# Moving part of a layer norm to GpSimd, one sum to VectorE, and the order of two stretches of work

## The reference, cut to what matters

```python
def _layernorm(x, axis=-1, eps=1e-05): ...          # no gain, no bias
def _binary_diff_weight(w, base):
    d = w - base
    coeff = jnp.mean(jnp.abs(d))                     # one number for the whole matrix
    return base + coeff * jnp.sign(d)
# FFN branch: 1792 inner columns in 14 chunks of 128
gate, up = xn @ W1.T, xn @ W3.T;  g = silu((silu(gate) * up) @ W2.T)
# attention-like branch: weights NF4[codes] * scales, rank 16 additions (LoRA)
attn = (q + k + v) / 3;  x1 = xn + o(attn);  s = x1 + down(silu(gate(x1)) * up(x1))
return x + s * g                                     # x: 1024 tokens x 512
```

## Time and profile before

| | |
|---|---|
| runs | 536.11, 536.21, 536.38 us; median 536.21 |
| the profiled execution | 536.4 us, span 534.6 us |
| PE busy | 522.1 us of the span, 98% |
| VectorE, ScalarE, GpSimd busy | 83%, 61%, 18% |
| mean granted clock of TensorE | 0.997 |
| PE's longest waits | 4.7, 1.7, 1.1, 0.9, 0.6 us |

### The profile page before, as it was taken

How to read it: one execution, slowest core, us unless ns; L and a number is a source line. 1 busy time by engine, 2 the same in 40 slices (tenths; PEclk the granted TensorE clock), 3 DMA queues, 4 the chain that set the end, 5 groups by cost and what they waited for, 6 DMA issues and landing times.

```text
span 534.6 us, 6499 instructions
## 1 busy us (share of the span) xinstructions
PE 522.1 (98%) x2337; PEld 432.2 (81%) x2337; DVE 442.0 (83%) x520; ACT 328.5 (61%) x455; POOL 94.8 (18%) x106
## 2 busy tenths in 40 slices
PE   5899999999999999999999999999999999999997
PEld 4678888888888888888888888887888888888886
DVE  6988998988896998865898988999989898874446
ACT  2979978557546555446648557867876585464310
POOL 1311002003100310022003121300310040004590
PEclk9899999999999999999999999999999999999999
DMA  8999904045811491059238994932582377127503
GB/s 337 397 402 403 377 4 154 25 132 99 189 50 63 70 229 58 1 104 224 51 75 159 243 219 100 195 83 63 97 163 58 75 157 148 29 51 161 135 20 139
DMA packets 31744, 76.73 MB, mean 144 GB/s; under 512 B 3872, under 2 KB 7296, under 8 KB 31584
## 3 DMA queue, kind: packets, MB, share of 16 engines
q1 hardware_dynamic: 21632, 57.42, 34.4%
q0 software_dynamic: 9792, 18.88, 20.4%
q10 hardware_dynamic: 288, 0.02, 0.0%
HBM read 53.23 MB, written 2.10 MB: 103 GB/s over the span
## 4 chain that ended last, share of the span: by engine, by line
PE 87%; DVE 8%; issue 3%; DMA 1%; ACT 1%; SPq 0%; DVEq 0%; ACTq 0%
PE up_ps L1692 25%; PE gate_pair L1692 22%; PE down_pair L1733 10%; PE up_ps L1733 9%; PE down_ps L1733 7%; PE side_ps L1776 2%; PE down_pair L1692 2%; DVE acc L1339 2%; PE down_pair L1645 1%; PE up_ps L1853 1%; PE gate_pair L1853 1%; PE down_pair L1853 1%; DMA xn<-in_x 1%; PE down_pair L1815 1%; PE gate_pair L1733 1%
## 5 line engine op out<-in xcount | busy, mean ns | idle before, releaser
L1692 PE MATMUL up_ps<-xT,gu 128*128 128x512 f32 x648 | 152.3, 390 | 0.4 <-DVE gu L1173 0.2
L1692 PE MATMUL gate_pair<-xT,gu 128*128 128x512 f32 x624 | 148.4, 390 | 0.0
L1692 PEld LDWEIGHTS up_ps<-xT,gu 128*128 128x128 f32 x648 | 121.4, 188 | 26.4 <-DVE gu L1173 0.6
L1692 PEld LDWEIGHTS gate_pair<-xT,gu 128*128 128x128 f32 x624 | 117.0, 188 | 24.6 <-DVE gu L1164 0.5
L651 POOL DMA_DIRECT2D y<-y_part x64 | 55.3, 875 | 339.9 <-ACT y_part L815 338.7
L802 ACT ACTIVATE h<-up_ps 128x512 fp32r<-128x512 f32 x52 | 31.0, 597 | 111.1 <-DVE up_ps L1231 58.0
L861 ACT ACTIVATE ramp<-codes,bend_bias 128x1536 f32<-128x1536 uint8 x56 | 88.1, 1579 | 0.9 <-DMA codes<-in_codes 0.9
L1339 DVE SCALAR_TENSOR_TENSOR acc<-ramp,acc 128x1536 f32<-128x1536 f32 x42 | 73.7, 1754 | 4.4 <-ACT ramp L861 4.0
L1733 PE MATMUL down_pair<-h,dn 128*128 128x512 f32 x249 | 60.9, 389 | 0.0
L1733 PEld LDWEIGHTS down_pair<-h,dn 128*128 128x128 f32 x249 | 46.7, 188 | 9.8
L1236 DVE TENSOR_TENSOR h<-up_ps,h 128x512 fp32r<-128x512 f32 x52 | 35.8, 689 | 19.7 <-ACT h L802 19.4
(11 more groups left out here) (227 smaller groups left out, 648.1 us busy)
## 6 DMA issues: line engine op xcount, KB each, us to landing
y<-y_part POOLq DMA_DIRECT2D x64, 256.0 KB, 5.0
scale<-in_scales SPq DMA_DIRECT2D x28, 384.0 KB, 5.5
scan_w<-in_w SPq DMA_DIRECT2D x15, 512.0 KB, 10.9
base<-in_mean SPq DMA_DIRECT2D x9, 768.0 KB, 4.8
scan_mean<-in_mean SPq DMA_DIRECT2D x9, 512.0 KB, 9.7
silu_gate<-in_mean SPq DMA_DIRECT2D x6, 512.0 KB, 12.2
codes<-in_codes SPq DMA_DIRECT2D x14, 192.0 KB, 5.6
xn<-in_x SPq DMA_DIRECT2D x4, 512.0 KB, 4.9
```

The lines of the kernel that those rows point to most:

```text
L1692: last = nc.tensor.matmul(ps[:, :], w[:, w_part, hc * P:(hc + 1) * P], xT[:, x_part, hc, th * HALF:(th + 1) * HALF], start=(hc == 0 and w_ ...
```

## The change

GpSimd normalises x tiles 4 to 7, after its copy of `next_gate` and ahead of `early_low`; it waits for the tenth `ln_step` and counts on a semaphore of its own. Scan tile 2 is summed by VectorE (`scan_sum(2)`) instead of ScalarE (`sum_apart(2)`). VectorE does scan tiles 0 and 1 back to back, then all eight low tiles. ScalarE makes the high part of the early base weight before the first scan tile. On PE the warm-up transposes have other counts and places, both halves of `early_signs` stand ahead of the first `total`, and chunk 2 of gate is made earlier. Late in the kernel, chunk 18's orders on VectorE and ScalarE change.

```diff
-DVE_SUMS = [4, 6, 8, 9, 12]
+DVE_SUMS = [2, 4, 6, 8, 9, 12]
-SUM_FIRST = [2, 3, 13]
+SUM_FIRST = [3, 13]
-WARM = {-1: 12, 1: 8, 3: 5, 7: 7}
+WARM = {-1: 8, 1: 8, 3: 7}
+WARM_LOW = {1: 3, 2: 3, 3: 3}
+WARM_TOTAL = [5, 8]
+H_AHEAD = [18]
+RANK_AHEAD = [18]
@@ GpSimd
+            pool.wait_ge(ln_step, 10)
+            for t in range(HC, TT):
+                nc.gpsimd.tensor_scalar(xn[:, t, :], xn[:, t, :], moments[:, t, 0:1], inv_std[:, t:t + 1],
+                                        ALU.subtract, ALU.mult).then_inc(xn_ready_pool, 1)
             early_low()
@@ ScalarE
+                if k in RANK_AHEAD:
+                    split(k)
                 steps(k, 1, 0, 1)
...
+                    if stage == "D4" and t == 6:
+                        y_evict(g, t)
+                        steps(stage, 1, 3, 4)
+                        continue
...
+            early_high()
             scan_signs(0)
-            early_high()
...
-            sum_apart(2)
...
+            unit_high(2)
             unit_signs(3)
             silu(0, 0)
-            unit_high(2)
@@ VectorE, phase(k)
+                if k - 1 in H_AHEAD:
+                    h_low(k - 1, 1)
+                    third_scale(k - 1)
...
+                if k in RANK_AHEAD:
+                    for s in NF4_STEPS[k - 1][1][2:3]:
+                        nf4_bend(s)
+                        nf4_scale(s)
+                else:
+                    rank_part(k)
...
+                if k in H_AHEAD:
+                    h_make(k, 1)
...
+                if k + 1 in RANK_AHEAD:
+                    rank_part(k + 1)
@@ VectorE, head
             scan_subtract(0)
-            for t in range(4, TT):
-                normalise(t)
             scan_subtract(1)
-            for t in range(4):
+            for t in range(TT):
                 x_low(t)
-            x_low(4)
-            x_low(5)
             scan_subtract(2)
-            x_low(6)
-            x_low(7)
+            scan_sum(2)
...
             early_scale(0)
+            unit_make(2)
             early_add(0)
             early_scale(1)
-            unit_make(2)
+            unit_low(2)
             early_add(1)
             scan_subtract(5)
-            unit_low(2)
@@ PE
+            pe.wait_ge(ln_step, 1)
             warm(side_ps, WARM[-1])
             for t in range(TT):
-                pe.wait_ge(xn_ready, t + 1)
+                if t < HC:
+                    pe.wait_ge(xn_ready, t + 1)
+                else:
+                    pe.wait_ge(xn_ready_pool, t - HC + 1)
...
-            pe.wait_ge(xT_lo, 1)
-            warm(early_ps[0], WARM[TT - 1])
+            for low, count in WARM_LOW.items():
+                pe.wait_ge(xT_lo, low)
+                warm(early_ps[0], count)
...
             early_signs(0)
+            early_signs(1)
+            warm(gate_ps[1], WARM_TOTAL[0])
             total(GATE)
-            early_signs(1)
+            warm(gate_ps[1], WARM_TOTAL[1])
```

More of the change, by code:

```diff
@@ L340, in block_kernel @@
         xn_ready = sem("xn_ready")
+        xn_ready_pool = sem("xn_ready_pool")
         xT_tr = sem("xT_tr")
@@ L883, in phase @@
                     silu(k, 0)
-                    split(k)
+                    if k not in RANK_AHEAD:
+                        split(k)
                 steps(k, 1, 1, 2)
@@ L928, in down_stage @@
                             dn_high(SPLIT_IN[stage])
-                    else:
+                    elif stage != "D4" or t != 5:
                         steps(stage, 1, t - 2, t - 1 if t < TT - 1 else None)
@@ L1377, in phase @@
             def phase(k):
-                if BEFORE[k] == k - 1:
+                if k - 1 in H_AHEAD:
+                    h_low(k - 1, 1)
+                    third_scale(k - 1)
+                elif BEFORE[k] == k - 1:
                     h_make(k - 1, 1)
-                    third_scale(k - 1)
+                    if k not in RANK_AHEAD:
+                        third_scale(k - 1)
                 make(k)
                 steps(k, 0)
-                if BEFORE[k] == k - 1:
+                if BEFORE[k] == k - 1 and k - 1 not in H_AHEAD:
                     h_low(k - 1, 1)
@@ L1386, in phase @@
                     dn_low(k)
-                rank_part(k)
+                if k in RANK_AHEAD:
[4 more added lines that the diff above has]
+                    rank_part(k)
                 if k == FIRST:
@@ L1395, in phase @@
                     return
-                steps(k, 1, 0, 1)
-                split(k)
+                if k in RANK_AHEAD:
+                    split(k)
+                    steps(k, 1, 0, 1)
+                else:
+                    steps(k, 1, 0, 1)
+                    split(k)
                 steps(k, 1, 1, 2)
@@ L1402, in phase @@
                     h_low(k, 0)
+                if k in H_AHEAD:
+                    h_make(k, 1)
                 for s in ATTN_STEPS[k][1][2:3]:
                     attn_step(s)
-                for s in NF4_STEPS[k][1][2:3]:
-                    nf4_bend(s)
+                if k + 1 in RANK_AHEAD:
+                    rank_part(k + 1)
+                else:
+                    for s in NF4_STEPS[k][1][2:3]:
+                        nf4_bend(s)
                 if k - 1 not in LATE_PHASES:
```

## The result

The changed kernel takes 542.48 us (542.29 to 543.36, 4 runs) against 536.16 (536.08 to 536.38, 4 runs): a ratio of 1.0121 [1.0106, 1.0135], 6.3 us slower. The forecast was 535.9, the range 534.6 to 537.6.

The account below looks back on a forecast made before the run. PE, which never pauses once chunk 1 of gate starts at 32.01, was taken as the bound. 536.4 + 0.1 (head) - 0.2 - 0.2 (two gaps) = 536.1, the median 0.2 below: 535.9 us, range 534.6 to 537.6.

Parts of the forecast that it names:

- The price of the normalise: Head, GpSimd: each normalise takes the copy's 0.6 us a tile, with the two-input operation's 1.28 as upper bound.
- my 32.15: Head, PE: forecast start of chunk 1 of gate, total at 29.9 plus a chain of 2.26, against 32.01 before.
- Case C: Head, GpSimd: a slow normalise of 1.28 us a tile, chunk 1 at 34.7, 538.5 us; chance 0.06.
- Blocking: Head: GpSimd's normalises and VectorE's scan subtracts lock each other out and queue, tile 7 ready at about 18.6.
- B: Head, PE: the clock falls to 1.2 GHz around 18 all the same, chunk 1 at 33.5, 537.3 us; chance 0.20.
- the 1.7 us: Head, PE: today's clock drop under early_mean costs about 1.7 us, which the change earns back.
- the floor at 31.0: Head: the last gate unit's landing lets chunk 1 start at 31.0 at the earliest, at most 1.0 us before today's.
- The signs ahead of the total: Head, PE: sign matmuls and transposes now ahead of the total cost 1.8 + 0.55 us.
- The two small gaps: PE's idle 0.21 us before 37.95 (chunk 2 of gate) and 0.19 before 370.12 (chunk 18) close, -0.2 each.

Follow-up runs that it names:

- clock_held: The changed kernel with 30 more transposes after tile 3 and 13 after each of tiles 4, 5 and 6; 540.66 us, ratio 1.0083.
- mul_add_held: The changed kernel with GpSimd's normalise written as multiply and add, and 22 more transposes after tile 3; 535.76 us, ratio 0.9992.
- late_and_chunk_2: The kernel before with only the late edits and the earlier making of gate's chunk 2; 535.53 us, ratio 0.9979.
- signs_after_total: The changed kernel with VectorE normalising tiles 4 to 7 and the second eight sign matmuls behind the total, without transposes around it; 535.66 us, ratio 0.9988.
- short_subtracts: The changed kernel with VectorE's scan subtracts 0 and 1 cut to 8 of 1024 columns; 541.1 us, ratio 1.0082.
- late_part_only: The kernel before with only the late edits (chunk 18's orders on VectorE and ScalarE, the moved ramp in D4); 535.34 us, ratio 0.9984.

## Why the prediction was wrong

**The price of the normalise: the step that failed.** I took 0.6 us from the copy, because both read one tile, and 1.28 as an upper bound, because the other operation reads two. It is 2.06. Reading one tile is no reason to be cheaper: the pair of operators sets the rate, 1.92 against 0.62. I should have held "no row shows this operation there" against any upper bound. The one TENSOR_SCALAR of GpSimd in the kernel before (128x96, 0.26 us) is multiply-add, and would have misled me the same way. The four took 10.33 us, 4 x 2.06 and 2.1 of waiting, where I had 4.6, 4 x 0.6 and 2.2 of waiting. So tile 7's transposes start at 24.38 and not at 18.7: 5.7 of the 7.0 us by which chunk 1 misses my 32.15. Case C had the right mechanism (0.06) and the same waiting, at 62% of the price and without the clock's loss.

**Blocking.** That they block was right, and the waiting was of the size forecast; that GpSimd slips in between two subtracts was not: by pointers it waited for the end of the whole series, in the change (4.16), with the fast form (2.73) and alone (5.09). By constants it got in after one (2.96, and VectorE's second subtract took 1.63).

**The clock.** B was right that it falls, and for the reason that it gave, thin work on PE: PE was idle for 3.54 us ahead of 18.21. Of the 7.0 us it is 1.7: 2.69 from tile 7's transposes to `early_mean` where I had 1.55, and 5.97 for `early_mean` where I had 5.45; the chain behind `total` gave 0.3 back (1.96 in place of 2.26). `clock_held` brings back 1.5. B's own price was near that, 1.35 in `early_mean`'s start (21.6 against 20.25).

**What a held clock is worth.** In the change's order the 1.7 us would have come: in `mul_add_held`, `early_mean` takes 5.55 from 20.95. In the order before they do not: in `late_and_chunk_2` PE waited 0.82 for tile 7's low part and reached the total at 29.31, only 0.44 before the 29.75 of the earlier trace rows; with VectorE's longer list of the change (`signs_after_total`) it waited 1.5 for the sums and got to it at 29.74. A faster PE met the next wait. For the same reason the floor at 31.0 was no gain of 1.0: the total of the up matrix, which I had not looked at, bounds PE next, at 50 to 51.

**The signs ahead of the total.** Held: in the change `total` is at 37.21 for sums ready at 34.7; in `mul_add_held` at 30.67 for sums ready at 29.97. With the clock held that is little, and putting them back changed nothing in the time (535.66 against 535.67), since PE then waits for the sums.

**The two small gaps.** Right in place, too small in size: 0.5 and 0.48 in place of 0.2 and 0.2, and a third, 0.31, left out. With the right form of the operation and the clock held the whole change is 535.76, 0.1 from the forecast. That is luck, for it comes by other terms: chunk 1 starts 0.6 later (32.63), not 0.1, and behind it 1.2 are gained, not 0.4.

## What to carry to other kernels

Price an operation on another engine by its own operators, or measure it in a probe that changes one thing at a time; an operation that looks like more work is no upper bound. Write a normalise for GpSimd as multiply-add. Read PE's gaps from start to start, and ask of every microsecond won on the first chain which sum or landing, two waits further on, takes it back.

## What the runs showed of the hardware

- GpSimd's tensor_scalar, 128x512: multiply-add, add-multiply and multiply-multiply 0.62; subtract-multiply and add-add 1.92; one operator alone 1.5. The Trainium skill, "GPSIMD Engine Reference", section "4.1 Engine selection", calls one-input work there roughly line-rate: multiply-add agrees (0.62 for 512, 1.04 for 1024 columns), subtract-multiply doesn't (2.07 and 3.78 by pointers). VectorE took 1.91 for four by pointers with either pair.
- A GpSimd operation with pointers stood until the end of a series of two-input VectorE operations in all seven profiles in which it met one, one with constants entered after one (3 of 3, a copy among them). Why is open. The Trainium skill, "SBUF — State Buffer", section "SBUF: two separate sides", has the lock as held for one instruction; short_subtracts agrees on the lock (4.16 against 2.08), and that a whole series keeps its turn the runs show beyond it.
- It works the other way too: VectorE's two-input low part of 0.68 us took 1.77 when a two-input subtract of GpSimd had started 0.08 us ahead of it (`late_and_chunk_2`, 34.34 and 34.42).
- VectorE's one-input operations on SBUF lengthen GpSimd's pointer form from 2.07 to 2.78 and are themselves 0.83 in place of 0.42 where they meet; with an input in PSUM neither is touched (4.24 for two).
- PE's idle time as shown leaves out some 0.3 us of a stop: 0.19 shown, 0.48 lost, and 0.78 us of time gained in `late_part_only` where 0.23 had been shown.
